# Graph network kernel: the gate's dot product as four multiply-and-sum instructions per quad instead of one product and one sum

## What is computed

```
edge_input = concatenate([x[src], edge_attr])                       # 96 + 32 features
messages   = gelu(edge_input @ mW1 + mb1) @ mW2 + mb2
gates      = sigmoid(gelu(edge_input @ gW1 + gb1) @ gW2 + gb2)      # gW2 has one column
aggregated = segment_sum(messages * gates, dst)
```

## Time and profile before

| | |
|---|---|
| median of three runs | 10923.42 us |
| profiled execution, span from first to last instruction (the page gives no other time for it) | 10933.0 us |
| edge loop, in which all quads run | from some 60 to some 5780 us of the span |
| PE busy over the span | 75% |
| POOL busy | 59% |
| DVE (VectorE) busy | 45% |
| ACT (ScalarE) busy | 25% |

### The profile page before, as it was taken

One profiled execution on the slowest core, in us unless ns is written; L12 is line 12 of the kernel. 1 busy time (PEld: TensorE's weight loads), 2 busy tenths in 40 slices (PEclk: granted clock), 3 DMA queues, 4 the chain that ended last, 5 costly groups with the idle time before them and its releaser, 6 DMA issues. The chain is left out here.

```text
span 10933.0 us, 150076 instructions
## 1 busy us (share of the span) xinstructions
PE 8192.3 (75%) x42144; PEld 5220.9 (48%) x42144; DVE 4899.6 (45%) x11836; ACT 2690.1 (25%) x6600; POOL 6435.5 (59%) x6424
## 2 busy tenths in 40 slices
PE   4777777777777777777777578887777577887776
PEld 4555555555555555555555233333334333433333
DVE  7666666666666666666667122222222121222222
ACT  3444444444444444444443000000000000000000
POOL 4555555555555555555554666666664666666663
PEclk7888888888888888888887788888887688888887
DMA  4444444444444444444444456666565465666656
GB/s 147 123 138 131 136 132 136 132 135 132 135 133 135 133 135 135 134 135 133 135 132 134 155 207 220 216 218 214 208 212 198 156 215 206 224 217 210 210 207 207
DMA packets 933049, 1818.03 MB, mean 166 GB/s; under 512 B 277359, under 2 KB 745600, under 8 KB 875312
## 3 DMA queue, kind: packets, MB, share of 16 engines
q10 hardware_dynamic: 65600, 773.65, 18.6%
q1 hardware_dynamic: 615456, 578.39, 16.9%
q0 software_dynamic: 251856, 464.10, 14.8%
HBM read 1361.12 MB, written 454.48 MB: 166 GB/s over the span
## 5 line engine op out<-in xcount | busy, mean ns | idle before, releaser
L962 POOL DMA_INDIRECT hid<-src_table,src_ids x3127 | 3136.7, 1003 | 2510.4 <-ACT msg L1358 1590.2
L1240 PE MATMUL bd<-ring,table_sb 128*96 128x480 f32 x6272 | 2941.6, 614 | 513.3 <-issue 511.7
L1240 PEld LDWEIGHTS bd<-ring,table_sb 128*96 128x96 f32 x6272 | 1071.7, 176 | 2131.6 <-issue 2131.1
L1007 POOL DMA_INDIRECT hid<-conv_table,hid x1596 | 1561.9, 979 | 751.1 <-issue 486.2
L1155 PE MATMUL sg<-hot,msg 128*98 128x64 f32 x6272 | 831.1, 286 | 1115.9 <-ACT msg L1358 1105.2
L1132 PE MATMUL bd<-one_hot_dst,one_hot_src 128*128 128x168 bf16 (+1 forms) x10368 | 1277.0, 274 | 253.5 <-issue 252.3
L1007 POOL DMA_INDIRECT feat_in<-conv_table,hid x1056 | 1026.1, 972 | 545.2 <-issue 324.6
L1155 PEld LDWEIGHTS sg<-hot,msg 128*98 128x98 f32 x6272 | 746.8, 199 | 1252.2 <-issue 1180.0
L1972 DVE TENSOR_TENSOR acc<-acc,sg 96x64 f32 x400 | 87.2, 218 | 2450.0 <-remote 1652.7
L1132 PEld LDWEIGHTS bd<-one_hot_dst,one_hot_src 128*128 128x128 bf16 x10368 | 1007.1, 110 | 299.1 <-issue 284.3
L1367 ACT ACTIVATE blocks<-bd 128x480 f32<-128x480 f32 (+1 forms) x1152 | 658.1, 571 | 1704.7 <-PE bd L1132 811.8
(11 more groups left out here) (248 smaller groups left out, 10307.8 us busy)
## 6 DMA issues: line engine op xcount, KB each, us to landing
ring<-adjacency ACTq DMA_DIRECT2D x448, 1680.0 KB
adjacency<-blocks SPq DMA_DIRECT2D x384, 980.0 KB
attr<-in_attr SPq DMA_DIRECT2D x392, 128.0 KB
hid<-src_table,src_ids POOLq DMA_INDIRECT x3127
hid<-conv_table,hid POOLq DMA_INDIRECT x1596
feat_in<-conv_table,hid POOLq DMA_INDIRECT x1056
conv_table<-table_sb SPq DMA_DIRECT2D x28, 336.0 KB, 2.4
feat_half<-feat_keep SPq DMA_DIRECT2D x56, 168.0 KB
```

The source lines that it names most:

```text
L962: pool.indirect_dma_start(out=hid[s][:, t, :], out_offset=None, in_=src_rows, in_offset=bass.IndirectOffsetOnAxis(ap=src_ids[h][:, j:j + 1 ...
L1007: pool.indirect_dma_start(out=conv_g[j][slot][:, t, :], out_offset=None, in_=conv_rows[l], in_offset=bass.IndirectOffsetOnAxis(ap=conv_ids ...
L1240: op = nc.tensor.matmul(side_ps[w].rearrange("r (o z) -> r o z", o=UNIT_OCTETS), table_sb[:, D * k:D * (k + 1)], ring[slot][:, :, OCTET_FA ...
```

## The change

`dot` loses its product and its sum over the quad, and the semaphore `s_prod` between them. In their place stand four `tensor_tensor_reduce` instructions, one for each tile: each multiplies 96 hidden values by the 96 weights, writes the products to `prod[:, t, :]` and their sum to one column of `logit`; the last raises `s_dotted`. As `s_prod` is gone, two more orderings are written out: `s_yz` gets a credit of 1 from SP, `build_part` waits for a value higher by that credit, and `pick_sides` waits on VectorE's own `s_yz` before it overwrites `side_now`.

```
+YZ_CREDIT = 1
...
-        s_prod = sem("gate_products")
...
+            sp.sem_inc(s_yz, YZ_CREDIT)
...
-                    pe.wait_ge(s_yz, nb * OCTET + QUAD * (q + 1))
+                    pe.wait_ge(s_yz, nb * OCTET + (QUAD * (q + 1) + YZ_CREDIT))
...
                 if not first:
                     dve.wait_ge(s_dotted, i)
-                v.tensor_tensor(prod[:, :, :], hid[s][:, :, D:H2],
-                                gate_w2_now.unsqueeze(1).to_broadcast([P, QUAD, D]), ALU.mult).then_inc(s_prod, 1)
-                dve.wait_ge(s_prod, i + 1)
-                v.tensor_reduce(logit[s % 2][:, :], prod[:, :, :], AX.X, ALU.add).then_inc(s_dotted, 1)
+                for t in range(QUAD):
+                    op = v.tensor_tensor_reduce(out=prod[:, t, :], in0=hid[s][:, t, D:H2], in1=gate_w2_now, scale=1.0,
+                                                scalar=0.0, op0=ALU.mult, op1=ALU.add,
+                                                accum_out=logit[s % 2][:, t:t + 1])
+                op.then_inc(s_dotted, 1)
...
                 dve.wait_ge(s_built, nb * PARTS + (BUILT_CREDIT - PARTS + 1))
+                dve.wait_ge(s_yz, nb * OCTET + YZ_CREDIT)
```

## The result

The changed kernel takes 11083.73 us (median of 4 runs, 11076.78 to 11092.75), the kernel before 10923.51 us beside it: ratio 1.0144, 95% interval 1.013 to 1.0158. That is 160 us more, above the range of the forecast (10880 to 11010 us). From the end of the first quad's weighing to the end of the last, the edge loop took 5627.5 us before and takes 5771.3 us now: 144 us of the 155 us by which the profiled span grew.

The account below looks back on a forecast made before the run. The prediction took a 14.26 us circle of PE and ScalarE per pair of quads, without DVE, as the bound; all terms were 0 but 2 us in the first four iterations, giving 10925 us, range 10880 to 11010 us.

Parts of the forecast that it names:

- Added instructions: DVE's dot product: four multiply-and-sums cost 1.16 us per quad against 1.06 removed, so the queue grows by 0.10 us.
- L1709's price: DVE: 0.22 us for 96 elements, from a two-operation instruction's step, plus 0.07 us to write out the sum.
- On-path cost: 0: Edge loop: DVE's +0.10 us per quad stays within margins of 0.61 and 1.2 us, covered by PE's round; cost 0.
- a saving would also end there: DVE in the edge loop: earlier tanh and gelu gain nothing, since the block copy behind them still waits for PE.
- a hold-up with no releaser: PE's order before 3031.31 us: ScalarE's block copy and DVE's addition, having waited about 2 us, start within 0.25 us.
- Rival B: POOL is the hidden bound; gathers no longer held by the long product save 67 us: 10858 us, chance 0.10.
- My evidence against B: POOL's gathers: 0.7 us of lateness in one run moved the pair by 0.14 us; POOL's pause takes it.
- Rival A: Multiply-and-sum above 0.42 us delays PE's attribute product through the addition; 157 us more, 11080 us, chance 0.15.
- the waits at 0: The added wait in pick_sides holds on arrival, and PE's higher value goes with the credit: both cost 0.
- a longer queue covered: DVE's longer queue lies under PE's round and costs 0; without that cover the bill would be 78 us.
- a pair that follows DVE's queue: Sign that the forecast is wrong: the time of a pair of quads moves up or down with DVE's queue.
- gathers whose mean length changes along with the pair's: Sign that the forecast is wrong: POOL's gathers change in mean length as the pair of quads does.

Follow-up runs that it names:

- 8: Kernel before with two gathers per quad instead of four in all iterations but the first of a round: 8980.31 us, ratio 0.8218.
- 9: Changed kernel with two gathers per quad instead of four: 8925.11 us, ratio 0.8174.
- run 7: Kernel before with an idle reduction (0.34 us per quad) behind its sum, making VectorE's queue longer: 10935.51 us, ratio 1.0006.
- 4: Kernel before with product and sum over 56 of 96 features, two old instructions made shorter: 10984.54 us, ratio 1.0053.
- run 3: Changed kernel with an idle reduction (about 0.34 us per quad) ahead of the four multiply-and-sum instructions: 11009.58 us, ratio 1.0072.
- 2: Changed kernel with an idle reduction (about 0.34 us per quad) behind the four multiply-and-sum instructions: 11012.4 us, ratio 1.0079.
- run 5: Kernel before with its product whole and its sum over 16 of 96 features: 10942.44 us, ratio 1.0014.
- run 1: Kernel before with only the change's two wait edits (YZ credit, wait in pick_sides): 10935.29 us, ratio 0.9998.
- 17: Changed kernel with bf16 elementwise output and an idle two-source product, which holds gathers, ahead of the four instructions: 10785.28 us, ratio 1.0014.
- 18: Changed kernel with bf16 elementwise output and an idle reduction over 128x192 elements, which holds no gather, as pad: 10823.53 us, ratio 1.0038.
- run 13: Kernel before, where POOL waits ahead of an odd quad's gathers until the even quad's have landed: 10734.26 us, ratio 0.9843.

## Why the prediction was wrong

**Added instructions: mis-sized, in the cheap direction.** I took 4 x 0.29 = 1.16 us; measured 0.71, so DVE's queue changed by -0.35 us per quad and not by +0.10. L1709's price was too dear a neighbour for a short instruction: 0.18 us for 96 elements with the read of the sum is nearly the low end (0.16). The sum's own record (80 ns, at the same start as the next multiplication) costs no step at all. The Trainium skill's rule of half rate for two SBUF sources that aren't bf16 with an accumulator ("Vector Engine (DVE) Microarchitecture Reference", "Points that are easy to get wrong") would have made it 0.39 us by my estimate; the rows don't show that for this instruction, whose step is 0.18 us.

**"On-path cost: 0" and "a saving would also end there": this step failed.** It took the pair's 14.26 us as a circle of PE and ScalarE in which DVE has no link, and left out why PE stood still before 3031.31. I had read that row, a hold-up with no releaser, and treated it as a fixed length. Runs 8 and 9 show that it isn't: with half the gathers the pair takes 9.30 us. PE slows down late in a run of eight and is free some 2.5 us after the last one starts. What part of PE's order has been done by then decides which block copy ScalarE stands at, and so whether tanh and gelu still have to follow (3046.02 to 3047.41). The term that I put at 0 measured +160 us, 0.4 us per pair. Lengthening DVE's queue did nothing (run 7, 1.0006), shortening it or taking its long product away cost 0.5 to 0.8% (runs 4, 3, 2), though only 0.14% where the long product stayed whole (run 5). I read this as a circle in which all engines stand, DVE too, and whose length is a fit and not a sum. By which link 0.35 us of DVE make PE slow down earlier in the pair is not shown.

**POOL: half right.** Rival B had POOL as the hidden bound, and runs 8 and 9 and the stops once per 104 gathers say that the pair does follow its run. But B's mechanism, gathers no longer held, gave the wrong sign: gathers of L963 did get shorter (987 ns for 1003 before), and the pair grew. The Trainium skill ("SBUF — State Buffer", "SBUF: two separate sides") says that a VectorE instruction with two SBUF inputs and a GpSimd operation that reads SBUF shut each other out for a whole instruction. The rows agree for the product (1.19 us against 0.95). But L1682 has two SBUF inputs too, and the 535 gathers that it overlaps by over 0.1 us take 0.95 us in the mean, so not every overlap holds a gather. What such a rule doesn't tell is that a hold may be worth having. My evidence against B, one run of eight with 0.7 us of lateness that cost 0.14 us, was a single pair. The same trace has counter-evidence, which I had missed: the stop once per 104 gathers, where 1.5 to 1.8 us of lateness cost 1.3 us in 27 of 28 pairs.

**Rival A: the time, not the mechanism.** It gave 11080 us for an instruction dearer than 0.42 us; that instruction costs 0.18 us. The attribute product's wait on the addition, its place, didn't become the bound.

**Right:** the waits at 0 (run 1), and a longer queue covered (run 7). Of my signs, "a pair that follows DVE's queue" and "gathers whose mean length changes along with the pair's" both came, the first with the sign turned round.

**What is shown and what isn't.** Shown: the loss is in the edge loop, in pairs mostly longer by 1 to 2.5 us; it isn't the two added waits nor DVE's load; it goes when the gathers are halved or when another wait bounds. Pointed at, by 4 against 5 (intervals 1.0028 to 1.0077 and 1.0004 to 1.0024) and 17 against 18 (whose intervals overlap): the long product, perhaps by its hold on the gathers, is part of what kept the lock. The first gathers differ by only 0.06 us in the mean between 4 and 5 and by 0.09 between 17 and 18. Open: what the rest is in the new instruction (its number of records, its own reads, or the wait on the products that went with it), what in the chip slows PE in a long run of gathers, why run 13 is faster, and why the change costs 2.4% on top of it, where no lock is. The clock's part is open too: in runs 4 and 5 PE spends 6.3 and 6.1 us of a long pair at the lower clock and 4.1 and 4.0 us of an equal one (from the clock records), and this may be a cause or come of the longer stand-still. A pad that holds gathers for as long as the old product, 0.55 us, was not tried, nor the change alone with bf16 output.

**A better version.** The kernel before with the pause of run 13, 10734 us, beats both. Its own runs spread from 10682 to 10828 us, all below the 10919 to 10950 us of the kernel before beside them. The change shouldn't be put on top of it (10995 us).

## What to carry to other kernels

A stand-still without a releaser is a term of the sum with an unknown cause; find what it moves with (here: halve the gathers) before you call anything beside it free. When nearly all rounds have the same length to 0.2 us, look at their distribution and not only at the mean, and ask what the odd ones out have in common: they are an experiment that the trace has already run. Such a lock can be lost by taking work away. "No engine waits for it" bounds what a longer instruction costs; it doesn't bound what a shorter one does.

## What the runs showed of the hardware that I had not expected

- In a run of gathers from GpSimd without a pause, matmuls start only one, or a few, per 0.7 to 1.4 us, from 7 to 10 us after its first (6.9 and 9.7 in the two pairs shown) until about 2.5 us after its last, at a granted clock of 1.00 and a DMA share of 0.29. Two gathers per quad in place of four: no such stretch, PE busy 97%, granted clock 1.00 for 0.86.
- GpSimd stops once per 104 gathers for 1.8 to 2.1 us, in both kernels.
- A multiply-and-sum over 128x96 f32 from two SBUF tiles has a step of 0.18 us; the record of 79 to 80 ns that writes the sum lies under the next one.
- 0.33 us more of idle work per quad on VectorE made a kernel 0.7% faster (run 3 against the change).
- Two chips ran the kernel before in 10775 us, the others in 10923 to 10939. The pairs of runs 17 and 18, made there, have a common length of 14.08 and 14.11 us for 14.27; the kernel before has no trace from them.
